# Last three slot tiles through a matrix product, the quotient behind the turned inputs in six pairs, two weight remainders on GpSimd

## The reference, cut to what matters

```python
dots = einsum('bhid,bhjd->bhij', q, k) * scale     # per sequence 256 x 768, 16 heads
out  = einsum('bhij,bhjd->bhid', softmax(dots), v) # then @ Wout
...
for e in range(8):
    h = gelu(x @ W1[e] + b1[e]); y = h @ W2[e] + b2[e]
    out = out + where(idx == e, y, 0)              # idx: one expert a token
x = x + tanh(g_ffn[1]) * out
```

## Time and profile before

| | |
|---|---|
| median of 3 runs | 711.27 us |
| the profiled execution | 712.78 us, of which its span is 710.8 us |
| TensorE matmul busy | 654.4 us, 92% of the span |
| VectorE busy | 526.7 us, 74% |
| ScalarE busy | 374.0 us, 53% |
| GpSimd busy | 348.4 us, 49% |

### The profile page before, as it was taken

One profiled execution on the slowest core, in us unless ns is written; L12 is line 12 of the kernel. 1 busy time (PEld: TensorE's weight loads), 2 busy tenths in 40 slices (PEclk: granted clock), 3 DMA queues, 4 the chain that ended last, 5 costly groups with the idle time before them and its releaser, 6 DMA issues.

```text
span 710.8 us, 14384 instructions
## 1 busy us (share of the span) xinstructions
PE 654.4 (92%) x5412; PEld 492.6 (69%) x5412; DVE 526.7 (74%) x1074; ACT 374.0 (53%) x581; POOL 348.4 (49%) x441
## 2 busy tenths in 40 slices
PE   5779999999999889899999999999999999799994
PEld 4656666665778777676677767777677777577884
DVE  5767888676488887798678787777889787857533
ACT  3656766666543444654455444644555355536652
POOL 3284444450044413566667566675657466661131
PEclk9779999999999999999999999999999999999998
DMA  8200000000200003000001000001100000120211
GB/s 187 26 0 2 2 2 1 3 2 1 100 23 1 0 1 112 1 1 1 2 1 31 16 1 11 21 16 31 31 2 2 1 2 23 49 60 12 67 50 56
DMA packets 35267, 16.96 MB, mean 24 GB/s; under 512 B 12824, under 2 KB 33648, under 8 KB 35072
## 3 DMA queue, kind: packets, MB, share of 16 engines
q1 hardware_dynamic: 33680, 14.94, 8.0%
q0 software_dynamic: 512, 1.05, 0.5%
q10 hardware_dynamic: 1008, 0.07, 0.1%
HBM read 12.05 MB, written 3.93 MB: 22 GB/s over the span
## 4 chain that ended last, share of the span: by engine, by line
PE 69%; DVE 21%; issue 6%; ACT 1%; DMA 1%; POOL 1%; SPq 0%; POOLq 0%; DVEq 0%; ACTq 0%
PE ps L1944 66%; DVE o L1642 3%; DVE pmax L1629 2%; PE ps L1955 2%; DVE mx L1312 2%; DVE kql L1617 1%; DVE pmax L1626 1%; DVE exm L1508 1%; POOL y_tok L727 1%; PE ps L2048 1%; DMA raw<-in_L_xattn_Wproj_dram 1%; PE ps L2600 1%; DVE wsel L1505 0%; DVE rt_y L1419 0%; DVE rt_t L1418 0%
## 5 line engine op out<-in xcount | busy, mean ns | idle before, releaser
L1019 ACT ACTIVATE p<-ps 128x1024 f32<-128x1024 f32 x96 | 96.5, 1024 | 148.1 <-PE ps L1944 148.1
L756 POOL TENSOR_TENSOR acc<-p 128x256 f32<-128x256 f32 x124 | 92.1, 773 | 75.9 <-ACT p L1019 75.9
L1944 PE MATMUL ps<-p,v 128*64 128x256 f32 (+1 forms) x1280 | 123.4, 384 | 1.7 <-DVE o L1643 1.2
L1944 PE MATMUL ps<-kqh 64*128 64x256 f32 (+1 forms) x640 | 110.6, 372 | 13.6 <-DVE pmax L1626 4.0
L762 POOL TENSOR_TENSOR acc<-acc,p 128x256 f32<-128x256 f32 x124 | 88.9, 749 | 56.3 <-ACT p L1019 56.3
L1626 DVE TENSOR_REDUCE pmax<-ps 128x2 f32<-128x1024 f32 x64 | 78.2, 1222 | 33.5 <-PE ps L1944 33.3
L1312 DVE TENSOR_REDUCE mx<-ps 128x1 bf16<-128x512 f32 x128 | 82.5, 687 | 26.6 <-PE ps L1944 26.0
L1944 PEld LDWEIGHTS ps<-p,v 128*64 128x64 f32 (+1 forms) x1280 | 66.1, 126 | 47.6 <-issue 15.3
L1944 PEld LDWEIGHTS ps<-kqh 64*128 64x128 f32 x640 | 62.0, 192 | 42.8 <-issue 34.1
L656 POOL TENSOR_SCALAR q<-qst,rmask 128x256 fp32r<-128x256 f32 x64 | 58.8, 937 | 59.4 <-ACT qst L779 59.4
L883 ACT ACTIVATE p<-ps 128x1024 f32<-128x1024 f32 x64 | 65.5, 1025 | 23.1 <-PE ps L1944 21.5
(11 more groups left out here) (320 smaller groups left out, 1441.2 us busy)
## 6 DMA issues: line engine op xcount, KB each, us to landing
w_raw<-in_L_ffn_W_dram SPq DMA_DIRECT2D x8, 256.0 KB, 2.7
ys_scratch<-y SPq DMA_DIRECT2D x22, 64.0 KB, 1.5
ctx_all<-in_ctx_dram SPq DMA_DIRECT2D x4, 256.0 KB, 5.7
raw_kv<-in_L_xattn_Wkv_dram SPq DMA_DIRECT2D x1, 1024.0 KB, 5.0
ctx_all<-in_L_ffn_W_dram SPq DMA_DIRECT2D x4, 256.0 KB, 3.7
w_raw_late<-in_L_ffn_W_dram SPq DMA_DIRECT2D x4, 256.0 KB, 3.8
xs_scratch<-xnA SPq DMA_DIRECT2D x1, 832.0 KB, 4.5
xs_rawA<-xs_scratch SPq DMA_DIRECT2D x3, 256.0 KB, 3.1
```

The source lines that it names most:

```text
L756: ins = pool.tensor_tensor(acc1[:, at], p1[:, s, 0, at], p1[:, s, 1, at], ALU.add)
L1019: act.activation(p1[:, g % 2, u, :], bank(2 * (n % 2), 2), ACT.Exp, scale=SCALE1).then_inc(a_exp1.sem, 1)
L1944: return pe.matmul(o, lhsT, rhs, start=start, stop=stop)
```

## The change

There are three edits.

**The last three slot tiles.** Tiles 19, 20 and 21 of the 22 (tiles 6 to 8 of set 1; `KEPT` = 3) no longer go through DRAM. Their rows of `ys_scratch` are zeroed early in the kernel by one more DMA of SyncE, and the gather of set 1 waits for its first six tiles only. For the tokens whose slot lies in the last three tiles, VectorE writes at tile 14 a diagonal matrix of slot numbers in bf16 for each of the two token tiles (`kept_rows`: one small operation and two of 128x128); TensorE spreads them over all partitions at tile 15 by one product with ones; VectorE compares that row with the slot numbers of each kept tile at tile 17 (`kept_turned`: three operations of 128x256 out of PSUM), which gives `kept_T`, a 0/1 matrix slots by tokens. Behind the last tile TensorE multiplies it with `y1` in six fp32 products of 128x128 into bank 7. The last x gets the gathered rows in one operation and then the product in two.

**The quotient.** In the six pairs with p = 3 or 4 of the first three sequences the multiplication of the quotient moves behind `proj_low(g + 3, 1)` and the turned context or latents. The reciprocal stays where it was.

**Two remainders.** `w2_low(0)` and `w2_low(1)` leave VectorE at pairs 29 and 30. GpSimd makes them in pair 31, between its first four additions and its second four, as four subtractions of 128x256.

```diff
+        KEPT, ROWS_SLOT, KEPT_SLOT = 3, 15, 17
+        KEPT_FROM = SLOT_TILES[1] - KEPT
...
+            sp.dma_start(ys_dram[1][KEPT_FROM * P:SLOT_TILES[1] * P, :].rearrange("(n p) d -> p n d", p=P),
+                         xnA[:, 0:1, :].to_broadcast([P, KEPT, P])).then_inc(s_zero.sem, 16)
...
-            for tile in range(6, SLOTS_ALL - 3):
+            for tile in range(6, SLOTS_ALL - KEPT):
                 slots_out(tile)
             for b in range(B - 1):
                 sp.wait_ge(d_xD.sem, b + 1)
                 sp.dma_start(out_v[b], x_of(b)).then_inc(s_out.sem, 16)
-            for tile in range(SLOTS_ALL - 3, SLOTS_ALL):
-                slots_out(tile)
...
+            pool.iota(kept_at[:, :], [[P, 3]], base=-KEPT * P // 2, channel_multiplier=1,
+                      allow_small_or_imprecise_dtypes=True)
...
             def gathered(z):
-                pool.wait_ge(s_ys[z].sem, 16 * SLOT_TILES[z])
+                pool.wait_ge(s_ys[z].sem, 16 * (SLOT_TILES[0], KEPT_FROM)[z])
...
                 ins.then_inc(g_acc.sem, 1)
+                if g == G1 - 1:
+                    for e in range(2):
+                        pool.wait_ge(a_ffnH.sem, E + e + 1)
+                        for c in range(0, FC, 2):
+                            ins = pool.tensor_tensor(w2_hl[:, e, c:c + 2, 1, :], w2_raw(e)[:, c:c + 2, :],
+                                                     w2_hl[:, e, c:c + 2, 0, :], ALU.subtract)
+                        ins.then_inc(g_wlow.sem, 1)
...
-                then(dve.reciprocal(o1[:, g % OS, :], bank(6)[:, NQ:2 * NQ]))
+                step(dve.reciprocal(o1[:, g % OS, :], bank(6)[:, NQ:2 * NQ]))
+
+            def divided1(g):
+                own()
                 dve.tensor_tensor(o1[:, g % OS, :], bank(6)[:, 0:NQ], o1[:, g % OS, :],
                                   ALU.mult).then_inc(d_o1.sem, 1)
...
+            def kept_rows():
+                far = float(-KEPT * P // 2 - 1)
+                then(dve.tensor_scalar(slot_kept[:, :], slot_f[:, 0:TQ], float(KEPT_FROM * P + KEPT * P // 2), far,
+                                       ALU.subtract, ALU.max))
+                for t in range(TQ):
+                    ins = dve.tensor_scalar(slot_diag[:, t, :], identb[:, :], slot_kept[:, t:t + 1], None, ALU.mult)
+                ins.then_inc(d_route.sem, 1)
+
+            def kept_turned():
+                dve.wait_ge(e_route.sem, e_route.after(2, 1))
+                for n in range(KEPT):
+                    ins = dve.tensor_scalar(kept_T[:, n, :], bank(7)[:, 0:NQ], kept_at[:, n:n + 1], None, ALU.is_equal)
+                ins.then_inc(d_route.sem, 1)
...
+                turning = b + 1 < B and p in (3, 4)
                 if g >= 1:
                     divide1(g - 1)
+                    if not turning:
+                        divided1(g - 1)
...
-                if g in W2_PAIRS:
-                    w2_low(W2_PAIRS.index(g))
+                if turning:
+                    divided1(g - 1)
...
             output1(SLOTS_ALL - 1)
+            dve.wait_ge(s_y_tok[1].sem, 16 * TQ)
+            then(dve.scalar_tensor_tensor(out=x_of(B - 1), in0=y_tok[:, TQ * (B - 1):TQ * B, :], scalar=G_F1,
+                                          in1=x_of(B - 1), op0=ALU.mult, op1=ALU.add))
+            dve.wait_ge(e_route.sem, e_route.after(2, 2))
             for t in range(TQ):
-                dve.wait_ge(s_y_tok[1].sem, 16 * TQ)
-                dve.scalar_tensor_tensor(out=x_of(B - 1)[:, t, :], in0=y_tok[:, TQ * (B - 1) + t, :], scalar=G_F1,
+                dve.scalar_tensor_tensor(out=x_of(B - 1)[:, t, :], in0=tok(bank(7), t), scalar=G_F1,
                                          in1=x_of(B - 1)[:, t, :], op0=ALU.mult, op1=ALU.add).then_inc(d_xD.sem, 1)
...
                 if tile == 0:
-                    pe.wait_ge(d_ffnL.sem, 2 * E)
+                    pe.wait_ge(d_ffnL.sem, 2 * E - 2)
+                    pe.wait_ge(g_wlow.sem, 6)
...
+                if tile == ROWS_SLOT:
+                    pe.wait_ge(d_route.sem, d_route.after(2, 1))
+                    mm(bank(7)[:, 0:NQ], onesb[:, :], slot_diag[:, :, :].rearrange("p t d -> p (t d)")
+                       ).then_inc(e_route.sem, 1)
             down1(SLOTS_ALL - 1)
+            pe.wait_ge(d_route.sem, d_route.after(2, 2))
+            for n in range(KEPT):
+                pe.wait_ge(d_y.sem, SLOTS_ALL - KEPT + n + 1)
+                for t in range(TQ):
+                    ins = mm(tok(bank(7), t), tok(kept_T[:, n, :], t), y1[:, SLOTS_ALL - KEPT + n, :],
+                             n == 0 and t == 0, n == KEPT - 1 and t == TQ - 1)
+            ins.then_inc(e_route.sem, 1)
```

More of the change, by code:

```diff
@@ L142, in flamingo @@
         iota_r = area.take("iota_r", [P, 1])
+        kept_at = area.take("kept_at", [P, 3])
         one_hot = tuple(area.take(f"one_hot{z}", [P, n + 1, E], BF16) for z, n in enumerate(TOKEN_TILES))
@@ L248, in flamingo @@
         xs_raw = [area.take("xs_rawA", [P, SLOT_TILES[0], P])]
+        area = Area(nc, at_kqh, at_kqh + 2 * 4 * (NK + NQ))
+        kept_T = area.take("kept_T", [P, 3, NQ])
+        slot_diag = area.take("slot_diag", [P, TQ, P], BF16)
+        slot_kept = area.take("slot_kept", [P, TQ])
         area = Area(nc, at_kqh + 2 * 4 * (NK + NQ), at_kql)
@@ L715, in scattered @@
             def scattered(z, of, tiles):
-                pool.wait_ge(s_zero.sem, 32)
+                pool.wait_ge(s_zero.sem, 48)
                 pool.wait_ge(d_route.sem, d_route.after(z, 4))
@@ L1811, in first_slot @@
                     if p == 0:
-                        dve.wait_ge(s_zero.sem, 32)
+                        dve.wait_ge(s_zero.sem, 48)
                         tokens_norm(xnA[:, 0:TQ, :], x_of(0), 0).then_inc(d_xnD.sem, 1)
@@ L1906, in _ @@
             divide1(G1 - 1)
+            divided1(G1 - 1)
             for tile in range(SLOTS_ALL):
@@ L1916, in _ @@
                     experts1(1)
+                if tile == ROWS_SLOT - 1:
+                    kept_rows()
+                if tile == KEPT_SLOT:
+                    kept_turned()
                 if tile >= 1:
```

## The result

The changed kernel takes 704.52 us (median of 4 runs, 704.39 to 704.60), against 711.07 for the kernel before on the same chip (710.81 to 713.49). The ratio is 0.989, with a 95% interval of 0.987 to 0.992: faster, by 6.6 us. The forecast was 704.3. Its profiled execution took 704.6 with a span of 702.8, against 712.78 and 710.8. One execution of the kernel before, on the chip of the experiments `routing_behind_maximum` and `filled_wait`, took 1046.83 us at a mean granted clock of 0.558 and is left out wherever times are compared.

A forecast was written before the change was run, and what follows sets the result against it. TensorE was taken as the bound, holding 69% of the chain, VectorE 21%. Terms -4.65 - 2.0 - 0.5 + 0.15 = -7.0 us against the median 711.27 gave 704.3 us, range 702.0 to 707.3.

The forecast's parts named there:

- The tail: After the last slot tile: the last residual waits for the six products, not the gather, and starts 4.65 us earlier.
- The quotient: Six turning pairs: moving the multiplication off the path gains 0.34 us each, 2.0 us in all.
- it holds VectorE for 0.34: First turning pair: the multiplication starts at 326.41 and the low half at 326.75, so moving it gains 0.34 us.
- the bound of 2.5: Upper bound of the quotient's gain: six times 0.42, the multiplication's length, 2.5 us.
- The remainders: Pair 29: removing the remainder gains about 0.5 us, bounds 0 and 1.25, set by GpSimd's fold; pair 30 gains nothing.
- The row that the prediction gave for it, at 614.21: Pair 29: an 8-column operation taking 0.72 us ends with GpSimd's fold, cited as agreeing with the shared-port rule.
- The product at tile 15: Slot tile 15: one added TensorE product of 256 columns costs 0.15 us, between 0.1 and 0.4.
- The sum: Whole kernel: tail, quotient, remainders and the product at tile 15 together give -7.0 us.
- 1.5 lower: Whole kernel: the median of the runs, 711.27, lies 1.5 us below the profiled 712.78; the forecast starts from that median.
- slower than before: Rival, last pairs: more idle time in one piece keeps TensorE's clock at half longer; 712.3 us at 16 us; chance 0.03.
- the case given for the high end: Range's high end, 707.3 us: gather 2 us late, lower bound of the remainders and half the quotient's gain.
- the clock dip goes too: Rival, near 622 to 626 us: TensorE's clock no longer falls, saving about 1.7 us more, 702.6 us; chance 0.15.

The follow-up runs named there:

- routing_behind_maximum: Changed kernel with the quotient last in all pairs but 24 and pair 30's routing operations behind the second row maximum: 701.32 us.
- filled_wait: Changed kernel with the quotient last in all pairs but 24 and twelve unread products in TensorE's wait before pair 31's last maximum: 699.91 us.
- two_kept: Changed kernel with two slot tiles kept back in place of three: 706.39 us.
- tail_only: Kernel before with only the edit to the last three slot tiles, without the quotient and remainder edits: 708.34 us.
- changed_again: Changed kernel measured again with no edit, on another chip: 703.87 us.
- four_remainders_gpsimd: Changed kernel with four experts' weight remainders on GpSimd in place of two: 705.39 us.
- quotient_only: Kernel before with only the quotient's multiplication moved in the six turning pairs: 708.51 us.
- remainders_late_vectore: Changed kernel with the two remainders on VectorE behind pair 31, ahead of the other six, in place of GpSimd: 705.38 us, one run.
- reciprocal_waited: Changed kernel with VectorE waiting for the reciprocal's end before the low half of the projection in the six turning pairs: 707.31 us.

## Why the prediction was right

The time and the range were right, and so was the path of each edit. Two terms of the sum were mis-sized, what differs from run to run at the start was not in it, and that the time came out so near was in part luck.

**The tail.** Predicted -4.65, measured -4.65 (5.82 to 1.17) in each run with three tiles kept. The order was right too: the gather was there first, and the six products ended last. The twelve instructions of the products take 1.57 from 698.33 on; the added residual takes 0.48 (predicted 0.61) and is over at 699.56, 0.34 before they are (699.90). That the gather comes just in time, as the delays of the earlier trace rows gave it, is shown by two_kept: one tile fewer costs 2.0.

**The quotient.** Predicted -2.0, measured -3.07. The step that failed is "it holds VectorE for 0.34", taken from the two starts at 326.41 and 326.75. The multiplication also needs the reciprocal's result, so a wait for VectorE's own last instruction stands ahead of it. The low half that now follows reads no such result and starts before the reciprocal has ended: 0.18 more in each pair, 1.08 in six. The run with that wait put back measures just this. Even the bound of 2.5 was too small. That the 0.7 of cover behind the multiplication is enough held.

**The remainders.** Predicted -0.5, measured -0.64 between kernels with the same clock, on the path foreseen: from M2, the row maximum over 128x2 that releases TensorE comes 8.76 later (615.81) in place of 9.39 (617.64). The fold starts 4.95 after M2 in place of 5.38, 0.43 earlier (predicted 0.47). The long operation beside GpSimd's fold is shown by its two lengths, 1.31 beside the fold and 0.23 after it. The Trainium skill (SBUF — State Buffer, Who interferes with whom) has VectorE with two SBUF inputs and GpSimd reading SBUF lock each other out for a whole instruction, and the trace agrees. The row that the prediction gave for it, at 614.21, is not such a case: `tiles_i` reads one tile. It took 0.72 beside the fold and 0.17 in the changed kernel, where it came ahead of the fold, so an operation with one SBUF input was held as well (0.72 and 0.17 again in tail_only and changed_again). And the 5.25 of four_remainders_gpsimd spans several of GpSimd's instructions, not one. GpSimd's subtractions took 0.71 each (predicted 0.73) and were hidden.

**The product at tile 15.** Predicted +0.15, measured +0.03 to +0.12, by M3 to M4 of the changed kernels (71.32 to 71.38 with three or two tiles kept) against 71.26 to 71.29 without.

**The sum.** At the same clock the edits come to 4.65 + 3.07 + 0.64 - 0.09 = 8.3, not 7.0. The two medians differ by 6.55 in the first measurement and by 7.24 on the chip of changed_again. The forecast of 704.3 came nearer than its terms by luck, because two errors met. From the profiled execution to its like the change took 8.2 (712.78 to 704.6) and not 7.0; but the step "1.5 lower" from there to the median did not hold, since the changed kernel's profiled execution is only 0.1 above its median. That 1.5 was spread between runs and nothing to be carried over.

Three smaller points of the prediction do not hold either. The 1.09 ahead of 618.91 was not TensorE's last wait before the fall: in the kernel before it waited 0.59 more ahead of 620.95 and 0.52 ahead of 621.76. In the rival "slower than before", 712.3 is 704.3 with 16 us at half clock added, not 16 us in all beside the 3 that were there. And the case given for the high end comes to 707.45 (1.65 + 0.5 + 1.0 above 704.3), just outside 707.3.

The rival "the clock dip goes too" names something that comes and goes between runs of one program. Of the 14 profiles of this study, two have the added products. Of the other twelve the clock fell near the last pairs in eight, and kept 1.00 in four: changed, quotient_only, four_remainders_gpsimd and remainders_late_vectore. The fall cost 1.5 in the kernel before (22.62 - 21.08), 2.7 in changed_again and 2.8 in tail_only. In the first profile its absence (-1.5) nearly made up for the slower start (+1.87), so the rival's 702.6 was missed though its condition was met.

What decides the clock at the start and near the last pairs stays open. A slow start went without a fall in three profiles of four, but reciprocal_waited had both.

## What to carry to other kernels

When an instruction is moved off a path, the wait for its input moves with it: count from the start of the instruction ahead of that wait, not from its own start. When results go out through DRAM and come back, keep the last few in SBUF and pick rows by a product with a 0/1 matrix, for just as many tiles as it takes until the gather of the rest ends first, and no more. When GpSimd takes work from VectorE, look at what VectorE reads from SBUF in the same stretch: four experts' remainders on GpSimd made one of VectorE's last 5.25 us. Where totals differ by under 1%, compare stage lengths between fixed marks at the same granted clock, since the clock alone moved totals here by as much as an edit.

## What was not expected of the hardware

Four products of 512 columns near the start took 3.75 us in this timeline of the changed kernel, and 1.96 in that of changed_again, the same program:

```profile
12.39 1.96 PE L1990 MATMUL ps<-ctxT,wt 128*128 128x512 f32 x4 [0.44 <-ACT ctxT L795]
```

The ratio, 1.91, is near that of the two clock levels, 1.2 and 2.4 GHz, but the granted clock in the windows around it is 1.00 in both, so the granted clock does not tell which rate TensorE had there, and the cause is not shown. Four of the 14 profiles had the slow start (changed, reciprocal_waited, four_remainders_gpsimd, remainders_late_vectore), and in them M1 came at 324.89 to 325.39, in all others at 321.19 to 323.28. The Trainium skill (TensorE: Matmul & The Clock Gate, What's actually happening) says that the number of slow products at a kernel's start varies between runs of one kernel; the two profiles of this program agree.

Products of 1.48 us that nobody reads, put where TensorE waited for VectorE, went with a clock that stayed at 1.00 and a stage 1.3 us shorter (21.76 to 20.44): added work on the engine that bounds the kernel did not lengthen it and, by the granted clocks of all eleven runs with such products, most likely shortened it.
